# Attention values kept with channels on partitions, divided there by their row sums, in place of three sets of transposes

## The reference

```python
x = x + attn(layernorm(x))            # causal self-attention, 1024 keys
x = x + xattn(layernorm(x), ctx)      # cross-attention, 77 keys of context
x = x + ffn(layernorm(x))             # gated, int8 fake-quantized, 704 hidden
# attention: softmax(q k^T / 4) v per head, heads merged, then @ Wo.T + bo
# ffn: h = fq(silu(g) * u), g and u from fq(x); fq scales by the max over the whole tensor
```

## Time and profile before

| | us |
|---|---|
| median of 3 runs | 989.03 (986.09 to 991.65) |
| span of the profiled execution | 989.7 |
| TensorE busy in it | 906.5 (92%) |
| DVE busy | 708.9 (72%) |
| ACT busy | 602.1 (61%) |
| POOL busy | 312.7 (32%) |

### The profile page before, as it was taken

The page is one execution under the profiler, slowest core; times in us unless marked ns, Lnnn a source line. Parts: engine busy times, 40 slices in busy tenths (PEclk is TensorE's granted clock), DMA queues, the critical chain, the costliest instruction groups (busy, mean ns, idle before and its releaser), DMA issues. The chain is left out here.

```text
span 989.7 us, 17256 instructions
## 1 busy us (share of the span) xinstructions
PE 906.5 (92%) x6014; PEld 442.7 (45%) x6014; DVE 708.9 (72%) x1466; ACT 602.1 (61%) x1121; POOL 312.7 (32%) x348
## 2 busy tenths in 40 slices
PE   4788899999999989999999999999999989989976
PEld 2424343446444624364435433554343554543344
DVE  3788875767866792877767747678675548687987
ACT  2233477764667577646677566366688734647975
POOL 1242216420331216521422056223421123303633
PEclk9877999999999999999999999999999999998999
DMA  5240111334222151111221304112210162114009
GB/s 163 93 130 8 52 54 59 75 79 49 89 73 86 36 167 51 62 33 36 95 85 31 128 25 116 49 33 76 91 64 3 43 189 87 46 43 159 13 1 191
DMA packets 83568, 73.42 MB, mean 74 GB/s; under 512 B 19244, under 2 KB 79788, under 8 KB 83484
## 3 DMA queue, kind: packets, MB, share of 16 engines
q1 hardware_dynamic: 78540, 68.58, 22.8%
q0 software_dynamic: 4256, 3.21, 2.5%
q10 hardware_dynamic: 688, 0.53, 0.2%
HBM read 19.81 MB, written 13.13 MB: 33 GB/s over the span
## 5 line engine op out<-in xcount | busy, mean ns | idle before, releaser
L777 ACT ACTIVATE probs<-psum 128x512 f32<-128x512 f32 (+1 forms) x608 | 314.7, 577 | 184.9 <-PE psum L972 181.7
L1144 DVE CUSTOM_DVE_ANT_0 junk<-psum,mask 128x640 bf16<-128x640 f32 (+3 forms) x256 | 253.4, 1022 | 62.8 <-PE psum L936 61.1
L698 POOL TENSOR_SCALAR_AFFINE_SELECT probs<-probs 128x512 f32<-128x512 f32 x128 | 81.3, 637 | 396.2 <-ACT probs L777 395.9
L972 PE MATMUL psum<-q_stack,k_stack 98*128 98x512 bf16 (+3 forms) x768 | 189.3, 332 | 7.5 <-DMA q_stack<-max_rows 3.4
L997 PE MATMUL psum<-probs,v_sb 128*17 128x512 f32 (+3 forms) x1536 | 160.2, 496 | 3.8 <-POOL probs L698 3.4
L1140 DVE TENSOR_REDUCE rowmax<-psum 128x4 f32<-128x512 f32 (+2 forms) x96 | 97.6, 1045 | 64.5 <-PE psum L930 64.1
L936 PE MATMUL psum<-k_stack,q_stack 96*128 96x512 bf16 (+3 forms) x512 | 129.0, 345 | 7.0 <-DVE rowmax L1144 4.7
L972 PEld LDWEIGHTS psum<-q_stack,k_stack 98*128 98x128 bf16 x768 | 63.1, 98 | 137.5 <-ACT probs L777 80.6
L896 PE MATMUL psum<-xnT,wT 128*128 128x512 f32 x192 | 91.4, 607 | 0.6 <-ACT xnT L742 0.3
L821 PE MATMUL psum<-wT,xnT 128*128 128x256 f32 x384 | 87.2, 384 | 0.5 <-ACT xnT L742 0.3
L821 PEld LDWEIGHTS psum<-wT,xnT 128*128 128x128 f32 x384 | 73.1, 193 | 12.5 <-ACT xnT L742 1.4
(11 more groups left out here) (182 smaller groups left out, 1246.8 us busy)
## 6 DMA issues: line engine op xcount, KB each, us to landing
q_stack<-q_parts SPq DMA_DIRECT2D x192, 64.0 KB, 2.6
k_stack<-k_parts SPq DMA_DIRECT2D x192, 64.0 KB, 2.6
xq_stack<-xq_parts SPq DMA_DIRECT2D x168, 64.0 KB, 2.6
xn<-in_x SPq DMA_DIRECT2D x8, 512.0 KB, 4.9
res<-in_x SPq DMA_DIRECT2D x4, 1024.0 KB, 6.9
out<-res SPq DMA_DIRECT2D x8, 512.0 KB, 2.9
normT_hbm<-xnT SPq DMA_DIRECT2D x6, 512.0 KB, 3.5
xf<-normT_hbm SPq DMA_DIRECT2D x6, 512.0 KB, 3.6
```

Of the source, the lines that this page charges most:

```text
L698: nc.gpsimd.affine_select(out=tile, in_=tile, compare_op=ALU.is_ge, fill=0.0, base=0, pattern=[[0, GH], [1, P]], channel_multiplier=-1).th ...
L777: nc.scalar.activation(probs[n % 2][:, heads * k:heads * k + heads, 0:cols], bank_a(s)[:, 0:heads * cols].rearrange("p (h n) -> p h n", h= ...
L972: last = nc.tensor.matmul(bank[:, cols * n:cols * n + cols], k_stack[:, slot, h, P * j:P * j + P], q_stack[:, slot, half, h, q0 - HALF * h ...
L1144: nc.vector.tensor_tensor_reduce(out=junk[D_STEPS.place(s) % 2][:, 0:keys], in0=bank_d(s)[:, 0:keys], in1=m.mask[:, T - keys:T], scale=1.0 ...
```

## The change

1. The values tile has each channel followed by a column of ones (VW = 32: value, 1, value, 1, ...). `pv` and `xy` so give for each head 32 rows: channel d on row 2d and the row sum, once more for each channel, on row 2d+1.
2. A DMA on SP's queue moves each kept 128x512 tile into `y_parts[layer]` of shape [128, 3, 1024]: the 64 value rows to plane c = g // 2, the 64 sum rows to plane 2, both on the partitions of their channels. There is one such DMA for each `keep` and each `xy`, 64 in all.
3. A new step `yn` for each layer, batch, plane c and half: DVE takes the reciprocal of the sum plane, 128x512, in place, and POOL multiplies the value plane by it, 128x512. There are 32 of them.
4. `yN`, `xyN` and `yT` are gone, with ACT's copies of `yT`. `o` reads `y_parts` directly and waits for POOL's two products of its half.
5. `fillers` is gone.
6. `y_sb` is one buffer of one half (in the space of a spent weight), the next `keep` waits for the former's DMA. The sum plane is shared by both c: the DMA for c = 1 waits for the product of c = 0. The ring of `rem` buffers goes from 4 to 3. The feed-forward weights `wgT`, `wuT`, `wdT` lie in the same memory as `y_parts` of the self-attention, so ACT's writes of them wait for the last `o` of it.
7. `mT` transposes all 128 columns of `negmax` in place of 64 or 32.
8. `PICKS` is another list, with new lanes "n" and "e" for `yn`. It is some 1890 letters and is not shown.

```diff
-VW = D + 1
+VW = 2 * D
+REMS = 3
...
-A_KINDS = ("s2", "xT", "yT", "q", "k", "mT", "xs2", "xy", "kx", "wT", "wdT", "wrow")
-D_KINDS = ("s1", "xs1", "o", "v", "yN", "xyN", "vx")
+A_KINDS = ("s2", "xT", "q", "k", "mT", "xs2", "xy", "kx", "wT", "wdT", "wrow")
+D_KINDS = ("s1", "xs1", "o", "v", "vx")
...
+def scaled_by_dve(s):
+
+    return False
...
+def scaled_values(layer, b, part):
+
+    return [("yn", layer, b, c, half) for half in halves(part) for c in range(CC)] if layer and b == B - 1 else \
+           [("yn", layer, b, c, half) for c in range(CC) for half in halves(part)]
...
+                if s[0] in ("keep", "xy"):
+                    layer, (_, b, g, half) = int(s[0] == "xy"), s
+                    c, tokens = g // 2, slice(half * HALF, half * HALF + HALF)
+                    if layer:
+                        sp.wait_ge(*a_emptied(s))
+                    else:
+                        sp.wait_ge(y_kept, KEEPS.upto(s))
+                    if c:
+                        sp.wait_ge(*scaled(("yn", layer, b, 0, half)))
+                    elif b:
+                        sp.wait_ge(*scaled(("yn", layer, b - 1, 1, half)))
+                        sp.wait_ge(d_full, D_STEPS.upto(("o", layer, b - 1, half)))
+                    sp.dma_start(y_parts[layer][64 * (g % 2):64 * (g % 2) + 64, c:CC + 1:CC - c, tokens],
+                                 xy_sb[half] if layer else y_sb).then_inc(y_moved[layer][half], 16)
...
+                if s[0] == "yn" and not scaled_by_dve(s):
+                    _, layer, b, c, half = s
+                    here = y_parts[layer][:, :, half * HALF:half * HALF + HALF]
+                    pool.wait_ge(inverted, SUMMED.upto(s))
+                    nc.gpsimd.tensor_tensor(here[:, c, :], here[:, c, :], here[:, CC, :], ALU.mult).then_inc(scaled_pool, 1)
...
                 if s[0] == "keep":
                     _, b, g, half = s
-                    n = VALUES.latest(s, lambda x: half in halves(x[3]))
-                    if n:
-                        act.wait_ge(d_full, D_STEPS.upto(VALUES.step(n - 1)))
+                    if KEEPS.place(s):
+                        former = KEEPS.step(KEEPS.place(s) - 1)
+                        act.wait_ge(y_moved[0][former[3]], 16 * MOVES[0, former[3]].upto(former))
...
                 if s[0] == "o":
                     _, layer, b, n = s
-                    pe.wait_ge(*a_emptied(("yT", layer, b, CC - 1, n)))
-                    project_rows(s, (3, 7)[layer])
+                    for c in range(CC):
+                        pe.wait_ge(*scaled(("yn", layer, b, c, n)))
+                    project_rows(s, y_parts[layer], (3, 7)[layer])
...
-                if s[0] in ("yN", "xyN"):
-                    layer, g, part = int(s[0] == "xyN"), s[2], s[3]
-                    many = 4 * len(halves(part))
-                    bank = bank_d(s)[:, 0:P * many].rearrange("p (t h d) -> p t h d", h=GH, d=2 * D)
-                    sums = rsum[2 * layer + g % 2][:, 0:many, :]
-                    link(nc.vector.reciprocal(sums, bank[:, :, :, D]))
...
+                if s[0] == "yn":
+                    _, layer, b, c, half = s
+                    here = y_parts[layer][:, :, half * HALF:half * HALF + HALF]
+                    dve.wait_ge(y_moved[layer][half], moved(layer, b, c, half))
+                    nc.vector.reciprocal(here[:, CC, :], here[:, CC, :]).then_inc(inverted, 1)
```

197 lines of the change are left out of this document (92 added, 105 removed).

## The result

The changed kernel takes 1065.14 us (median of 4 runs, 1063.12 to 1069.34) beside 987.56 for the kernel before in the same call: a ratio of 1.0775, interval 1.0743 to 1.0808. The prediction said 983 and its range ended at 1012. It was wrong in size and in sign.

A forecast was written before the change was run, and what follows sets the result against it. The prediction took TensorE to bound the middle, and DVE with the chain of steps the tail. Middle -14, head 0 and tail +8 took the profiled 989.7 to 983.7, 0.7 above the median, so 983 us; range 955 to 1012.

The forecast's parts named there:

- The middle, stage by stage: From 100 to 795 us: the longer of TensorE and DVE per stretch leaves a gain of 3 to 25 us, 14 taken.
- Transposes, 43 us in the middle: TensorE's middle: 304 of the 384 removed transposes at 0.14 us give about 43 us, real if nothing else fills up.
- The reciprocal, 3.4 us: On DVE: each of 32 reciprocals of 512 elements takes 3.4 us, between 0.69 and 4.7; DVE's net is +75 us.
- Wider values, nothing: On TensorE: pv loading 32 columns of weights in place of 17 costs nothing, covered by the matmul that streams meanwhile.
- POOL, nothing: On POOL: 32 added products of 1.17 us, 37 us, cost nothing in the middle; without cover up to 1.2 us each.
- The moves on SP, nothing, up to 10: On SP's queue: 64 new DMAs of 256 KB landing in 2.6 us cost nothing, up to 10 us for the range.
- the fifth case: Moves make a new wait, each of 64 holding ACT or SP 0.3 us: +19, 1002 us; chance 0.05.
- The tail, +8: Last batch's second attention, from 795 to 891.5 us: 6 - 1 + 1 - 2 + 4 = +8 us.
- The clock's term: In the tail: a fifth of some 22 us of TensorE's chain work at 1.2 GHz costs +4 us.
- The fourth case: The tail goes cold, all 22 us of TensorE on the chain at 1.2 GHz: +20 in place of +4, 999; chance 0.13.
- The third case: DVE becomes the bound in clumps and tail, with reciprocals of 3.9 to 4.7 us: 1002 at 4.3 us; chance 0.12.
- The second case: The middle follows TensorE, DVE's lateness absorbed or long reciprocals faster: middle -41, tail +3, 951 us; chance 0.20.

The follow-up runs named there:

- e17: Kernel before with a copy of 64 elements of each bank in place of each division's reciprocal and multiply on DVE: 987.52 us, ratio 0.9989.
- e5: Kernel before with 24 reciprocals of 128x512 of a constant added on DVE, in pairs behind every second division: 1064.79 us, ratio 1.0777.
- e14: Kernel before with 24 reciprocals of 128x512 added on DVE singly, one behind each division of batches 0 to 2: 1076.06 us, ratio 1.0900.
- e15: Kernel before with 24 reciprocals of 128x256 added on DVE, one behind each division of batches 0 to 2: 1024.14 us, ratio 1.0365.
- e2: Changed kernel with each reciprocal over 32 of its 512 columns, the other sums left undivided: 1000.81 us, ratio 1.0140.
- e6: Changed kernel with reciprocals and moves both of 32 columns in place of 512: 969.87 us, ratio 0.9797.
- e12: Changed kernel with moves of 32 columns in place of 512 and full-length reciprocals, taken of a constant 1: 1040.88 us, ratio 1.0566.
- e16: Kernel before with each bank of value transposes written by one matmul of ones in place of four transposes: 984.38 us, ratio 0.9932.
- e1: Kernel before with its 102 idle matmuls left out and nothing else changed: 996.46 us, ratio 1.0082.
- e13: Changed kernel with short reciprocals and short moves, plus idle matmuls behind the last keep: 974.23 us, ratio 0.9881.
- e4: Changed kernel with idle matmuls put back behind the last keep only: 1062.92 us, ratio 1.0751.
- e11: Changed kernel with 1/sum taken on ACT as exp(-ln) in place of DVE's reciprocal, plus idle matmuls behind the last keep: 1102.86 us, ratio 1.1156.
- e3: Changed kernel's steps on the order of the kernel before, each yn some 8 us of TensorE's work behind its last move: 1284.63 us, ratio 1.3001.

## Why the prediction was wrong

**The step that failed** is "The middle, stage by stage". It cut both lists into stretches of 25 and 50 us, took the longer engine in each, "so that DVE may run late and catch up", and came to a gain of 3 to 25 us. It had no term for the granted clock of the middle. The middle grew by 50. DVE's work in the kernel before is hidden, and taking some away gives nothing (e17). But what is added to it costs 0.9 to 1.1 us for each us (e5, e14, e15), and in the changed kernel some 0.7 (64 to 71 us for 96: e2, e6, e12). The timeline of e5 shows why DVE can't run late: TensorE gets 0.9 us past the point where DVE is held, until it wants a bank pair and everything behind that in its list stands too. The place at 212 us shows a second way, by POOL's product and mask. DVE's 30% of idle time lay mostly in waits for TensorE (some 225 of 281 us of the whole kernel before) and couldn't be used to work ahead.

The second half of the cost is the clock. In us, from 100 to the last `pv`, one trace each; the last column is the sum over windows of 5 us, an estimate:

| run | last `pv` ends at | TensorE idle | lost to a lower clock |
|---|---|---|---|
| before | 796.2 | 28 | 2 |
| after | 846.4 | 78 | 46 |
| e2, short reciprocals | 788.2 | 45 | 24 |
| e6, short reciprocals and moves | 764.5 | 37 | 6 |
| e12, short moves | 821.5 | 68 | 32 |
| e5, pairs of reciprocals added | 876.3 | 78 | 34 |
| e14, singles added | 875.7 | 70 | 41 |
| e15, half as long | 828.4 | 45 | 19 |

The added idle time of e5 (50 us) is less than the 80 us of DVE that were added; with 32 of lower clock it comes to the 80 by which its last `pv` is later. So near one for one is a sum of two parts and no law of the ring, and a sum over shorter stretches without the clock would have come out too low as well. That is worked out from the traces; no run changed the clock of the middle by itself.

**How the 78 us add up.** Nearly free reciprocals and moves leave 970 (e6), 20 under before. The reciprocals' own 3.0 us over the short ones cost 64 to 71, the moves 24 to 31, together 95 (1065 - 970). The gain of 20 is what is left of the 53 us of transposes.

**Transposes, 43 us in the middle, "real if nothing else fills up".** Right in work, wrong in worth. Of the 20 us that e16 gave to TensorE, 6 came back in the median. By that share the 43 would have given some 13, close to the 14 of the forecast. That the 14 came out near is luck, since it was reached by DVE's load, while e16 lost the rest to idle time and a lower clock.

**The reciprocal, 3.4 us.** Right: 3.34. In pieces of 128 columns it is 0.93, so (3343 - 926) / 384 = 6.3 ns an element, the slope of the earlier trace rows. The Trainium skill, "VectorE: DVE Perf Modes", "First, the fixed hardware budget", with its repeat count of 8 led to an estimated 4.3 us. The measurement decides for the trace's slope, and as I read it with six steps of about 1.04 ns. DVE's net of +75 was right too (783.2 - 708.9 = 74.3).

**Wider values, nothing.** `pv` of 512 columns is 107.3 us in place of 102.8, in windows of which some are cold. Idle time before it rose to 8.4; 5.1 of this is the place at 222 us, which waited for POOL's mask, and 2.1 is put down to POOL in other places. I see no cost of the width.

**POOL, nothing.** Wrong. The products take 1.27 us, as forecast, but POOL stands 202 us in front of them for the reciprocals, and masks queue behind. The prediction saw that queue and priced only the product's own 1.2 us. At 212 us the mask was held until 222.0, and a `pv` with it for 5.1 us. In the middle TensorE stood 16 us for POOL, 7 of them in front of `o`, in place of 3 before. No run took this wait away by itself. The sum plane shared by both c also makes SP wait for the products (88 us in two rows of SP's waits, above). How much of the moves' 24 to 31 us is this wait and how much the landing was not parted.

**The moves on SP, nothing, up to 10.** Wrong: 24 to 31 us. The landing was taken from the row of 64 KB, and is 4.1 us at 256 KB where I took 2.6. DVE, whose time is dear, stands idle for them (18.0 and 15.4 us in the groups above, 11.7 of it in one place of the tail). With short reciprocals the full moves add 8 us of idle time and 18 of lower clock to the middle (e2 beside e6). Here the fifth case had the mechanism, at +19, with a chance of 0.05.

**The tail, +8.** It is +25: 120.1 us (846.4 to 966.5) in place of 95.3 (796.2 to 891.5). The chain at its start, forecast at 7.8 us and at -1 beside before, shows in the timeline of TensorE and DVE behind the last `pv`:

```profile
847.24 3.62 PE L855 MATMUL psum<-wT,y_parts 128*128 128x256 f32 x16
856.21 5.13 PE L855 MATMUL psum<-wT,y_parts 128*128 128x256 f32 x16 [5.35 <-POOL y_parts L716]
...
851.41 3.35 DVE L1182 RECIPROCAL y_parts<-y_parts 128x512 f32<-128x512 f32 x1 [11.74 <-DMA y_parts<-wT]
```

From the end of the last `pv` at 846.4 to the second `o` at 856.2 it is 9.8 us, of which DVE was waiting for the move until 851.4. That second `o` ends 14.9 us behind the last `pv`, where it was 14.1 before, and the first `xs1` begins 31.2 us behind it, where it was 31.7. So the start is not what made the tail longer. From there to the end of the last `xy` it is 58.6 us in place of 46.1, and from that to the feed-forward part 30.3 in place of 17.5. The end, first before (TensorE), then after (TensorE, ACT, DVE):

```profile
872.89 1.06 PE L1006 MATMUL psum<-v_sb,xv_now 77*32 77x512 f32 x8
878.37 3.62 PE L821 MATMUL psum<-wT,xnT 128*128 128x256 f32 x16
```

```profile
935.11 1.07 PE L1033 MATMUL psum<-v_sb,xv_now 77*32 77x512 f32 x8
951.62 5.22 PE L855 MATMUL psum<-wT,xy_parts 128*128 128x256 f32 x16 [4.92 <-POOL xy_parts L716]
...
942.12 0.60 ACT L832 ACTIVATE xy_half<-psum 128x512 f32<-128x512 f32 x1 [6.17 <-DMA xy_parts<-xy_half]
...
946.82 3.35 DVE L1182 RECIPROCAL xy_parts<-xy_parts 128x512 f32<-128x512 f32 x1 [3.40 <-DMA xy_parts<-xy_half]
```

From the last `xy` to the last `o` it was 4.4 us and is 15.4. The prediction put +1 on this. It has one copy, move, reciprocal and product in it; the trace has two moves in a row, since the last copy stood 6.2 us for the move of the `xy` before it, whose buffer it needs. In e6 the end is 21.7 us, so short reciprocals and moves give back 8.6 of its 12.8. The 12.5 us in the scores they do not: that stretch is 57.7 us in e6 too. By e1 (50.1) and e13 (53.2, warm) the clock has a part in it, and the rest stays open.

The clock's term had the right sign (0.68 there), and little weight: e4, e11 and e13 warmed the tail and gained 2.5 us at most, though leaving the idle matmuls out of the kernel before cost 8 (e1). The fourth case names the right sight and the wrong cause. (Its 22 us on the chain are four `o` and two q projections of 3.7 us each, and not "as much again" of the latter.)

**The cases.** The third case, DVE as the bound, had the right engine with the wrong price. It was tied to a reciprocal of 3.9 us and more, and by its own sum a reciprocal of 3.34 would have been no loss. The second case, a middle that follows TensorE, falls. Of the signs named ahead, waits of tens of us at SP's moves came true; TensorE didn't stay at 96% through the middle but fell to 90%, by waiting; with 43 us of work gone it would be lower still, had the lower clock not made the rest longer.

**What stays open.** Which part of the move's cost is landing, SP's queue, POOL's masks or the shared sum plane; what the new order is worth by itself, since e3 changed SP's queue too; why the scores of the tail take 12 us more; and what sets the time of the kernel before. The lower clock in the middle (46 us by the windows) was never taken away by itself. No version that computes the whole layer was faster than the kernel before.

## What to carry to other kernels

When one engine is 96% busy and another empties its ring of two buffers, the second engine's idle time is no slack: price what you add to it at 0.7 to 1.1 us for each us, though taking the same work away may give nothing. Average loads, and maxima over stretches much longer than the ring, hide this; look instead for how far the full engine gets after the other is held. Then count the gaps once more for the clock: here it took about as much as the gaps that the change added. And ask what stands in each engine's list behind a new wait, as the masks did behind POOL's product. When a bracket names a releaser that the program does not wait for, read the line of the wait itself.

An operation whose cost goes by the elements of a partition wants its data without repetition: with each sum written 16 times a reciprocal is 3.34 us long, where the 32 sums of a partition in the old layout cost 0.36.

## What the runs showed of the hardware

- The reciprocal on DVE costs 5.9 to 6.3 ns for each element of a partition, taken between the lengths seen: 0.36 us for 32, 0.93 for 128, 1.74 for 256, 3.34 for 512, beside 0.69 for a multiply of 512.
- A move of 256 KB between tiles lands in 4.1 us, one of 16 KB in 1.9. The kernel before shows 2.6 for 64 KB.
- A power on POOL takes 81.9 us for 128x512, some 65 times the product of the same form (1.27):

```profile
L719 POOL TENSOR_TENSOR y_parts<-y_parts,unread 128x512 f32<-128x512 f32 x16 | 1311.1, 81945 | 34.5 <-DMA y_parts<-wT 34.5
```

- Each switch between Ln and Exp on ACT loaded a table for 1283 ns, 64 times.
- More gaps on TensorE came with a lower clock: with 28 us of idle time in the middle it took an estimated 2 us, with 70 to 78 us of idle time 34 to 46 (table above).
- Giving TensorE less to do may lower its granted clock a little. In e16 the middle had 6 windows of 5 us of 138 under 0.95, and the lower clock took 8 us. The kernel before had 1 of 140 and e1, the same program up to the last `pv`, 3 of 139 (2 and 3 us).
